# Softmax's division moved from GpSimd into the transposing product: a diagonal matrix of reciprocal row sums

## The reference, cut to what matters

```
scores = jnp.einsum('bhsr,bhlr->bhsl', q_r, k_r)
attn = jax.nn.softmax(scores, axis=-1)
ctx_c = jnp.einsum('bhsl,bld->bhsd', attn, kv_r)
```

## Time and profile before

| what | value |
|---|---|
| median of 3 runs | 658.96 us (657.79 to 659.67) |
| the profiled execution's own time | 655.62 us |
| its span | 653.8 us |
| setup, to the first `x_turn` | 0 to 116.5 us of the span |
| stages 0, 1, 2, 3 | 116.5 to 236.8, to 367.7, to 500.6, to 603.3 us |
| output product, routing and experts of the last batch | 603.3 to 653.8 us |

### The profile page before, as it was taken

The page is one execution under the profiler, slowest core; times in us unless marked ns, Lnnn a source line. Parts: engine busy times, 40 slices in busy tenths (PEclk is TensorE's granted clock), DMA queues, the critical chain, the costliest instruction groups (busy, mean ns, idle before and its releaser), DMA issues.

```text
span 653.8 us, 8556 instructions
## 1 busy us (share of the span) xinstructions
PE 540.6 (83%) x3032; PEld 339.6 (52%) x3032; DVE 411.6 (63%) x806; ACT 248.4 (38%) x674; POOL 307.6 (47%) x300
## 2 busy tenths in 40 slices
PE   2862676868797679899999899999997999999696
PEld 1752334545454557555555575555554766554442
DVE  3999793479667536976864569768644353534244
ACT  1842221232433223543344334433442245354143
POOL 3765344259739713263345532542455224345466
PEclk9985898899999799999999998999998999999799
DMA  7940100012202200000000000000000000000000
GB/s 288 408 146 14 51 0 5 1 65 97 97 33 97 90 0 21 1 5 1 2 1 1 17 1 2 1 2 1 0 1 1 17 2 2 1 1 1 17 1 16
DMA packets 10201, 24.56 MB, mean 38 GB/s; under 512 B 4464, under 2 KB 6512, under 8 KB 9264
## 3 DMA queue, kind: packets, MB, share of 16 engines
q1 hardware_dynamic: 9920, 23.24, 9.9%
q0 software_dynamic: 240, 0.79, 0.3%
HBM read 22.97 MB, written 1.05 MB: 37 GB/s over the span
## 4 chain that ended last, share of the span: by engine, by line
PE 52%; DVE 27%; POOL 7%; ACT 6%; issue 6%; DMA 1%; SPq 0%; POOLq 0%; DVEq 0%; ACTq 0%
PE s L512 13%; PE qc L512 11%; PE ga L512 10%; PE qb L512 10%; PE ua L512 6%; DVE wk L1062 4%; DVE top L1060 3%; PE tp L515 2%; ACT reg L857 2%; DVE amax L987 2%; DVE reg L1134 2%; POOL reg L1375 2%; DVE nmax L1141 2%; POOL wE L1421 1%; DVE masks L1212 1%
## 5 line engine op out<-in xcount | busy, mean ns | idle before, releaser
L1375 POOL TENSOR_TENSOR reg<-reg,rsum 128x512 f32<-128x512 f32 x64 | 68.3, 1089 | 129.7 <-DVE rsum L1148 129.7
L857 ACT ACTIVATE reg<-s,nmax 128x256 f32<-128x256 f32 x128 | 59.0, 476 | 45.8 <-DVE nmax L1141 45.8
L1212 DVE SCALAR_TENSOR_TENSOR masks<-s,route,masks 128x256 f32<-128x256 f32 x120 | 51.5, 477 | 38.5 <-PE s L512 38.3
L512 PE MATMUL s<-wE,xhi 128*128 128x512 fp8e4 x192 | 73.6, 383 | 1.3 <-ACT reg L857 0.9
L512 PE MATMUL s<-wE,xlo 128*128 128x512 fp8e4 x192 | 73.5, 383 | 0.0
L512 PE MATMUL qc<-reg,wM 128*64 128x256 f32 (+1 forms) x384 | 68.6, 396 | 2.8 <-DVE reg L1134 2.8
L515 PE MATMUL tp<-idn,reg 128*128 128x128 f32 x248 | 39.8, 283 | 31.8 <-POOL reg L1375 16.0
L512 PE MATMUL qb<-reg,wA_hi 128*128 128x256 f16 x384 | 64.6, 278 | 1.5 <-ACT reg L842 1.4
L779 ACT COPY reg<-tp 128x512 f32<-128x512 f32 (+1 forms) x56 | 32.0, 572 | 67.8 <-PE tp L515 67.8
L1141 DVE TENSOR_REDUCE nmax<-s 128x2 f32<-128x512 f32 x64 | 40.9, 680 | 22.7 <-PE s L512 22.7
L512 PEld LDWEIGHTS qc<-reg,wM 128*64 128x64 f32 (+1 forms) x384 | 37.2, 153 | 31.6 <-issue 21.8
(11 more groups left out here) (192 smaller groups left out, 1094.6 us busy)
## 6 DMA issues: line engine op xcount, KB each, us to landing
masks<-in_moe_masks SPq DMA_DIRECT2D x16, 512.0 KB, 3.3
wM<-in_att_wq SPq DMA_DIRECT2D x1, 2048.0 KB, 7.7
wE<-in_wo_t SPq DMA_DIRECT2D x1, 2048.0 KB, 11.2
reg<-in_kc_q SPq DMA_DIRECT2D x1, 1536.0 KB, 10.9
reg<-in_qr_t SPq DMA_DIRECT2D x1, 1536.0 KB, 18.3
xb<-in_x SPq DMA_DIRECT2D x4, 256.0 KB, 3.4
wU<-in_gate_w SPq DMA_DIRECT2D x1, 1024.0 KB, 12.9
wD<-in_up_w SPq DMA_DIRECT2D x1, 1024.0 KB, 14.9
```

The source lines that it names most:

```text
L512: return nc.tensor.matmul(dst, lhsT, rhs, start=start, stop=stop, skip_group_check=not check)
L857: nc.scalar.activation(attn[p % 2][:, k * S:(k + 1) * S], s.tensor[:, (k % 2) * S:(k % 2 + 1) * S], ACT.Exp, bias=nmax[:, o:o + 1], accum_ ...
L1212: ins = nc.vector.scalar_tensor_tensor(acc[:, t, chain], src, w, acc[:, t, chain], ALU.mult, ALU.add)
L1375: nc.gpsimd.tensor_tensor(a, a, rsum[:, o + 2 * hh:o + 2 * hh + 2].unsqueeze(2).to_broadcast([P, 2, S]), ALU.mult).then_inc(attn_ready.sem, 1)
```

## The change

GpSimd's `attention` is gone. Behind the reciprocal, VectorE now builds `diag`: four 128x128 blocks, each the identity times one column of `rsum`. `attn_turn` no longer transposes by the identity; it is a plain product whose stationary operand is the tile of unnormalised attention and whose moving operand is the diagonal block, so that the tile comes out both turned and divided by its row sums. The semaphore that `attn_turn` waits for is now set by VectorE once per pair, not by GpSimd once per head. The scratch space for DMAs that GpSimd issues is set to 8192 bytes, which makes room for `diag`.

```
+        diag = sb("diag", 4 * P)
...
-        attn_ready = count("attn_ready", 2 * PAIRS)
+        diag_ready = count("diag_ready", PAIRS)
...
             def attn_turn(b, p, hh):
-                pe.wait_ge(attn_ready.sem, attn_ready.at(b, 2 * p + hh + 1))
+                pe.wait_ge(diag_ready.sem, diag_ready.at(b, p + 1))
...
-                        last = turn(k.tensor[:, c * S + t * P:c * S + (t + 1) * P],
-                                    attn[p % 2][:, (2 * hh + t) * S + c * P:(2 * hh + t) * S + (c + 1) * P])
+                        last = mm(k.tensor[:, c * S + t * P:c * S + (t + 1) * P],
+                                  attn[p % 2][:, (2 * hh + t) * S + c * P:(2 * hh + t) * S + (c + 1) * P],
+                                  diag[:, (2 * hh + t) * P:(2 * hh + t + 1) * P])
...
                 nc.vector.reciprocal(rsum[:, o:o + 4], ssum[:, o:o + 4]).then_inc(rsum_ready.sem, 1)
+                dve.wait_ge(rsum_ready.sem, rsum_ready.at(b, p + 1))
+                nc.vector.tensor_tensor(v3(diag[:, :], 4), idn[:, :].unsqueeze(1).to_broadcast([P, 4, P]),
+                                        rsum[:, o:o + 4].unsqueeze(2).to_broadcast([P, 4, P]), ALU.mult)\
+                    .then_inc(diag_ready.sem, 1)
...
-            def attention(b, p):
-                o = 4 * (p % 2)
-                pool.wait_ge(rsum_ready.sem, rsum_ready.at(b, p + 1))
-                for hh in range(2):
-                    a = v3(attn[p % 2], 4)[:, 2 * hh:2 * hh + 2]
-                    nc.gpsimd.tensor_tensor(a, a, rsum[:, o + 2 * hh:o + 2 * hh + 2].unsqueeze(2).to_broadcast([P, 2, S]),
-                                            ALU.mult).then_inc(attn_ready.sem, 1)
...
                 for p in range(PAIRS):
-                    attention(b, p)
...
-    nc = _bacc.Bacc("TRN2", target_bir_lowering=False, num_devices=1)
+    nc = _bacc.Bacc("TRN2", target_bir_lowering=False, num_devices=1, dynamic_dma_scratch_size=8192)
```

## The result

The changed kernel takes 668.1 us (median of 4 runs, 667.35 to 668.72) against 658.9 us for the kernel before in the same comparison (657.79 to 659.67). The ratio is 1.014, with a 95% interval of 1.0122 to 1.0158: 9.2 us slower.

The account below looks back on a forecast made before the run. TensorE was taken to bound stage 1, with GpSimd's division mostly beside the path. Stage 0's halves at 0 and -3.5, then +4.8, +4.8 and +3.2, sum to +9.3 us: 668 us, range 661 to 679.

Parts of the forecast that it names:

- The product: TensorE's attention turns: a plain product costs 0.46 us more per head than transposes, 29.4 us over 64 heads.
- the rival with 84 us: TensorE's attention turns: product costs four times a transpose, 84 us, some 60 showing, about 730 us; chance 0.02.
- What covers it: Waits behind the turns hide part of the product: 1.8 and 0.4 us in stage 1, 2.8 in stage 3.
- One sign: Profile after, stages 1 to 3: TensorE's waits for the attention nearly vanish.
- Nothing is covered: Waits behind the turns move along; stages 1 to 3 cost 7, 7, 6, stage 0 +2: 681 us; chance 0.17.
- The diagonal: VectorE, one 128x512 multiplication per pair: 0.73 us with the wait, 23.4 us in all, 5.8 a stage.
- the cover in stage 0's first half: Three diagonals, 2.2 us, precede VectorE's statistics, against some 2.7 us these lay waiting for GpSimd.
- What GpSimd's division had cost: Head 0's 1.09 us wait becomes 0.73, head 1's second 1.09 goes; stage 0's quantisation loses 6.7 us of contention.
- The first half: Stage 0 to 178.6 us: diagonals, longer turn and later quantisation against shorter waits and less contention sum to 0.
- The second half: Stage 0, pairs 5 to 7: diagonals +2.2, turns +0.9, less contention -6.7; sum -3.6, rounded to -3.5.
- Stages 1 to 3: Longer turns and diagonals less what waits cover: +4.8 us in stage 1, +4.8 in stage 2, +3.2 in stage 3.

Follow-up runs that it names:

- with GpSimd held back: The changed kernel, but GpSimd still waits for each pair's reciprocal where its multiplication stood, then does nothing: 679.3 us, ratio 1.0325.

## Why the prediction was right, point by point

**The product.** Right in kind and price: two records for a product, 0.89 us for four against 0.44, TensorE's busy time up by 26.8 us in the four stages where I said some 29. The Trainium skill, "TensorE: Matmul & The Clock Gate", section Terms, speaks of a factor of four for float32 with transpose mode; the trace shows two, and the rival with 84 us falls.

**What covers it.** Right. TensorE's waits inside stage 3 of the changed kernel, beside the earlier trace rows:

```profile
PE s L513 <- DVE masks L1218: 1.0, 6, 0.2
```

The same six places wait 1.0 us instead of 4.1, 0.5 less each: the longer turn lies in the wait. In stages 1 and 2 the four waits of `scores` for ScalarE's `tern`, 2.3 us a stage, are gone from the list. A price of 29 us shows as 12.2, 12.5 and 14.5 in three experiments. The waits just named account for 3.1 + 2 x 2.3 = 7.7 us of the difference, and stage 0, where at most 1.4 of 7.4 us show, for another 6 to 7. One sign was not met: TensorE's waits for the attention were to nearly vanish in stages 1 to 3, and 1.9 us for the diagonal remain in each of stages 1 and 2. "Nothing is covered" is refuted by the kernel before with products, 671.2 us and not 682.

**The diagonal.** The duration was right, the sum not. It takes 0.69 us in stages 1 to 3, and 6.87 / 8 = 0.86 on average in stage 0, where mask steps lie beside some. Pair 4 shows it, on VectorE:

```profile
178.79 1.30 DVE L1152 TENSOR_TENSOR diag<-idn,rsum 128x512 f32<-128x512 f32 x1
```

and on GpSimd:

```profile
177.05 5.39 POOL L1419 TENSOR_TENSOR wE<-masks,tern 128x512 fp8e4<-128x512 f32 x4
```

I had written that GpSimd would be idle at most of these times and took the low end; in stage 0 it is not. The mis-sized term is the cover in stage 0's first half: three diagonals "against some 2.7 us for which they lay waiting for GpSimd". The chains show the FFN's first product 60.0 and 59.5 us after the stage's start in the two kernels without a diagonal and 62.6 and 63.9 in the same two with it, so the first half pays 2.6 to 4.4 us for it. Measured alone, the diagonal costs 7.5 to 8.3 us in stage 0 and 13 to 15 in the whole kernel. In the expectations written after the result, I still allowed it 8 in the whole (668 less 660). Not all of the 7.5 to 8.3 is the diagonals' own time: the chain of the changed kernel holds 4.6 us of them, and in both kernels with a diagonal the first FFN product ran slowly (3.12 and 3.27 us, not 1.72), which a kernel with the same diagonals did not show (below).

**What GpSimd's division had cost.** Mis-sized by nearly as much the other way: 18.5 us by experiment with transposes and 16.3 with products (671.2 less 654.9), where I allowed 13 (659 less 646). TensorE's waits for it do not show the contention on VectorE, nor the mask steps behind it. So the net number was right with both of these terms too small: what the sum needed was their difference, and the diagonal instead of GpSimd's division gave 3.3 us with transposes and 3.1 with products. That the total came within 0.2 us of the forecast is luck. The experiments find this; the result alone would not have.

**Stage 0's halves.** The first half was to change by 0. In the chain, the FFN's first product started 62.1 us after the stage's start before (178.62 - 116.5) and 63.9 after (181.31 - 117.4), and took 3.27 us instead of 1.72 for the same four, at the lower clock: +3.3. The chain of waits of the changed kernel at both places:

```profile
178.79 1.31 DVE diag L1152
181.31 3.27 PE ga L513 x4
184.58 1.86 PE ua L513 x4
...
225.04 3.62 PE ga L513 x16
```

The later fours of this FFN take 1.72 us; the one behind the wait for the diagonal is slow. That wait alone does not make it slow, as the chain of the kernel with the diagonal in stage 0 alone shows, whose stage 0 has the same code:

```profile
179.27 1.31 DVE diag L1164
181.78 1.72 PE ga L518 x4
```

The same wait stands ahead of it, and the product takes 1.72 us. The place of the slow product belongs to the execution, then. A loss of this kind that kernel had too, only earlier: its FFN product started 65.4 us after the stage's start, not 63.9, behind slower products at the head of the stage (4.02 us against 3.32 for the first eighteen), and the stage came out as long, 116.9 us. The second half was to give 3.6 and gave 5.7. There the contention is gone as forecast. VectorE's windows over the operations that the earlier trace rows show:

```profile
197.99:201.20 3.21, 3.14 (x4) 1.00 0.00 0
212.96:217.50 4.54, 4.36 (x6) 1.00 0.01 4
```

3.14 and 4.36 us against 5.47 and 8.66 before, the values that I had taken from idle places. The last FFN product took 3.62 us instead of 5.23: in the kernel before, the windows from 225 to 229 us show a granted clock of 0.50 and 0.66, and 1.00 in the changed one. These are 1.6 us that I had not counted and that happen to pay for the 1.6 lost above. Among the experiments the same product took 3.62 to 4.71 us. The Trainium skill, "SBUF — State Buffer", section Who interferes with whom, says that a VectorE instruction with two SBUF inputs contends with a GpSimd instruction that reads SBUF; the trace agrees, with 2.17 us against 1.23 for the same operation (L1008, with GpSimd held back and in the changed kernel).

**Stages 1 to 3.** +4.9, +4.5, +3.9 against +4.8, +4.8, +3.2. The agreement is of single executions; the experiments split these sums by engine only as far as their table goes.

**What stays open.** How much of stage 0's differences between kernels is the clock. Each kernel was profiled once, and the granted clock in stage 0 went from 0.85 to 0.97 between kernels. Why ScalarE's division everywhere comes out 5.6 us dearer than in stage 0 alone (655.3 against 649.7 us) is open too: in the profiled executions stages 1 and 2 together differ by less than 1 us, stage 3 by 2.1, and 3.4 lie in stage 0, where the code is the same.

## What to carry to other kernels

Before a transpose is turned into a product to fold a scaling in, count the records that a plain product of that type leaves in the trace: in float32 it cost twice a transpose. Look for the engine that has room at the very place, not on average: in stage 0 the diagonal on VectorE cost some 8 us, GpSimd's division 11 and ScalarE's none to 3, while in the later stages GpSimd's was cheaper than ScalarE's (649.7 against 655.3 us in the whole) and than the diagonal with its product (655.1 against 668.1). And an edit whose number comes out right still wants its terms measured apart; here two were too small by 3 to 7 us each and met in the sum.

## What the runs showed of the hardware

A float32 product with 128 columns is two records of about 0.11 us from start to start, with the identity as with the diagonal (0.89 us for four products), and a float32 transpose one (0.44 us for four). On VectorE a multiplication of 128x512 took 0.69 us with GpSimd idle, and up to 1.75 beside mask steps; the masking behind the top-k rounds (L1072) took 0.48 us in the changed kernel and 1.30 with GpSimd held back; each instruction of the top-k rounds kept its 0.41 us in both. The granted clock dropped to its lower level behind some waits of TensorE and not behind others of the same length: products of 1.7, 2.1 and 3.6 us took 3.3, 3.7 and 5.2, at places that differ between kernels with the same code there.
